# DLRM tower with a CIN stack on one core: six and four weight groups in odd tiles, all first-layer groups split, first-layer schedule moved

## What is computed

```python
def _cin_layer(X0, Xi, W, b):              # X0 [B,39,16], Xi [B,Fi,16], W [128, 39*Fi]
    Wr = W.reshape(H, F0_, Fi)
    return jnp.einsum('hjk,bjd,bkd->bhd', Wr, X0, Xi) + b[None, :, None]
X0 = e                                     # rows of 39 tables, gathered by ids
Xi = X0
for W, b in Ws:                            # three layers
    Xi = _cin_layer(X0, Xi, W, b)
    res.append(Xi.sum(axis=2))
z = jnp.concatenate(res, axis=1)           # [B, 384]
h = jnp.concatenate([z, dense_ctx], axis=1)
h = jnp.maximum(h @ W_top1 + b_top1, 0.0)
h = jnp.maximum(h @ W_top2 + b_top2, 0.0)
y = h @ W_top3
```

## Time and profile before

| | |
|---|---|
| Time, median of 3 runs | 663.59 us (663.03 to 664.0) |
| The profiled execution's own time | 664.12 us |
| Its span, first to last instruction | 662.2 us |
| Mean granted TensorE clock | 0.995 |
| TensorE busy | 648.3 us |
| VectorE busy | 558.7 us |
| GpSimd busy | 467.0 us |
| ScalarE busy | 441.9 us |

### The profile page before, as it was taken

How to read it: one execution, slowest core, us unless ns; L and a number is a source line. 1 busy time by engine, 2 the same in 40 slices (tenths; PEclk the granted TensorE clock), 3 DMA queues, 4 the chain that set the end, 5 groups by cost and what they waited for, 6 DMA issues and landing times.

```text
span 662.2 us, 11304 instructions
## 1 busy us (share of the span) xinstructions
PE 648.3 (98%) x3070; PEld 517.9 (78%) x3070; DVE 558.7 (84%) x1558; ACT 441.9 (67%) x1449; POOL 467.0 (71%) x376
## 2 busy tenths in 40 slices
PE   7898999999999999999999999999999999999998
PEld 6786678777788777777778877877778877777877
DVE  4669999999985799999995699999998489999980
ACT  3555678677763777777773577868675477777761
POOL 6888788888873688888875468787886377444540
PEclk9799999999999999999999999999999999999999
DMA  6023564040403004031221301313040300400000
GB/s 212 18 50 100 137 231 129 20 121 8 127 10 116 17 7 126 8 101 37 78 59 35 99 6 32 106 23 115 18 121 8 113 18 8 125 3 6 1 1 1
DMA packets 38356, 42.25 MB, mean 64 GB/s; under 512 B 17823, under 2 KB 22548, under 8 KB 38165
## 3 DMA queue, kind: packets, MB, share of 16 engines
q1 hardware_dynamic: 32661, 40.23, 20.0%
q0 software_dynamic: 5632, 1.31, 2.2%
HBM read 8.84 MB, written 0.00 MB: 13 GB/s over the span
## 4 chain that ended last, share of the span: by engine, by line
PE 94%; DVE 2%; DMA 2%; ACT 1%; issue 1%; POOL 1%; SPq 0%; POOLq 0%; DVEq 0%
PE p_u L820 22%; PE p_u L822 22%; PE p_u L821 22%; PE p_x L795 6%; PE p_tower L843 5%; PE p_g L834 5%; PE p_x L790 2%; PE p_x L789 2%; PE p_x L792 2%; DMA g_all<-w_in 1%; DVE z L611 1%; PE p_tower L870 1%; PE p_x L760 1%; PE p_x L772 1%; PE p_g L748 0%
## 5 line engine op out<-in xcount | busy, mean ns | idle before, releaser
L461 ACT ACTIVATE prod<-p_u,x0t 128x128 f32<-128x128 f32 x1024 | 290.4, 375 | 104.1 <-PE p_u L822 104.0
L652 DVE SCALAR_TENSOR_TENSOR parts<-p_u,x0t,parts 128x128 f32<-128x128 f32 x1024 | 283.9, 342 | 42.2 <-PE p_u L822 42.0
L820 PE MATMUL p_u<-w1h,x1h 128*128 128x512 f32 (+1 forms) x640 | 288.4, 451 | 0.8 <-ACT x1h L442 0.8
L822 PE MATMUL p_u<-w1h,x1l 128*128 128x512 f32 (+1 forms) x640 | 250.4, 391 | 0.0
L821 PE MATMUL p_u<-w1l,x1h 128*128 128x512 f32 (+1 forms) x640 | 250.1, 391 | 0.0
L339 POOL DMA_INDIRECT emb<-table_in,idx_all x176 | 205.6, 1168 | 49.8 <-issue 47.7
L358 POOL TENSOR_TENSOR parts<-parts,prod 128x512 f32<-128x512 f32 x128 | 176.9, 1382 | 53.3 <-ACT prod L461 39.9
L820 PEld LDWEIGHTS p_u<-w1h,x1h 128*128 128x128 f32 x640 | 120.9, 189 | 37.9 <-issue 8.2
L821 PEld LDWEIGHTS p_u<-w1l,x1h 128*128 128x128 f32 x640 | 121.5, 190 | 35.6 <-issue 10.8
L822 PEld LDWEIGHTS p_u<-w1h,x1l 128*128 128x128 f32 x640 | 120.7, 189 | 26.1
L353 POOL TENSOR_TENSOR parts<-prod 128x512 f32<-128x512 f32 x64 | 83.4, 1302 | 73.1 <-ACT prod L461 72.4
(11 more groups left out here) (87 smaller groups left out, 383.0 us busy)
## 6 DMA issues: line engine op xcount, KB each, us to landing
fac_b<-xx SPq DMA_DIRECT2D x90, 234.0 KB
fac_a<-xx SPq DMA_DIRECT2D x45, 78.0 KB
emb<-table_in,idx_all POOLq DMA_INDIRECT x176, 3.7
g_all<-w_in SPq DMA_DIRECT2D x3, 832.0 KB, 6.3
w<-w_in SPq DMA_DIRECT2D x1, 2496.0 KB, 9.2
xx<-xx SPq DMA_DIRECT2D x30, 78.0 KB
fac_b<-xx SPq DMA_DIRECT2D x15, 156.0 KB
bd<-x0t SPq DMA_DIRECT2D x120, 10.0 KB
```

The costliest lines, as they stand in the source:

```text
L461: last = nc.scalar.activation(dst[:, i * H:(i + 1) * H], u[:, i * H:(i + 1) * H], ACT.Copy, scale=x0t[:, par, t, j:j + 1])
L652: nc.vector.scalar_tensor_tensor(out=chain[i][:, p], in0=u[:, i * H:(i + 1) * H], scalar=x0t[:, par, t, j:j + 1], in1=add, op0=ALU.mult, o ...
L820: nc.tensor.matmul(u, xh, wh, start=True, stop=False)
L822: nc.tensor.matmul(u, xl, wh, start=False, stop=True).then_inc(u_full, 1)
```

## The change

It makes three moves.

- **Odd tiles are wide.** In odd tiles from T = 5 to T = 61 (29 tiles) ScalarE scales six quads (0, 2, 4, 5, 7, 9) and VectorE four (1, 3, 6, 8). `prod` gets a fifth buffer for them, GpSimd adds four times instead of three, and all counters become sums over tiles (`A_DONE`, `V_DONE`, `SUMS_DONE`).
- **All seven groups are split**, so groups 1, 3 and 5 too are handled in halves from macro 2 on.
- **The slots of the first layer move**: products to 0, 4, 8, ... 24, high halves 4 slots behind, low halves 6, adds 10 (10, 14, ... 34). The last add stays in slot 34.

```diff
-S_PAIR = [1 + 9 * k // 2 for k in range(GROUPS)]
-S_HIGH = [s + 1 for s in S_PAIR]
-S_LOW = [s + 3 for s in S_PAIR]
-S_ADD = [s + 6 for s in S_PAIR]
-SPLIT = (0, 2, 4, 6)
+S_PAIR = [4 * k for k in range(GROUPS)]
+S_HIGH = [s + 4 for s in S_PAIR]
+S_LOW = [s + 6 for s in S_PAIR]
+S_ADD = [s + 10 for s in S_PAIR]
+SPLIT = tuple(range(GROUPS))
...
-CHAIN_TILE = 20
-A_TILE = 5
-SUM_TILE = 3
+WIDE = [T % 2 == 1 and TILES < T < TILES_BLOCK * BLOCKS - 1 for T in range(TILES_BLOCK * BLOCKS)]
+A_QUADS = [(0, 2, 4, 5, 7, 9) if wide else (0, 2, 4, 6, 8) for wide in WIDE]
+V_QUADS = [(1, 3, 6, 8) if wide else (1, 3, 5, 7, 9) for wide in WIDE]
+A_DONE = [sum(map(len, A_QUADS[:T])) for T in range(len(WIDE) + 1)]
+V_DONE = [4 * sum(map(len, V_QUADS[:T])) for T in range(len(WIDE) + 1)]
+SUMS = [len(A_QUADS[T]) - 2 for T in range(len(WIDE))]
+SUMS_DONE = [sum(SUMS[:T]) for T in range(len(WIDE) + 1)]
+PRODS = [4, 5]
...
-        prod = sb("prod", [128, 2, 4, 4 * H])
+        prod = sb("prod", [128, sum(PRODS), 4 * H])
...
-                    pool.wait_ge(a_scaled, A_TILE * T + 3)
+                    pool.wait_ge(a_scaled, A_DONE[T] + 3)
...
-                    for i in (2, 3):
-                        pool.wait_ge(a_scaled, A_TILE * T + 2 + i)
-                        pool.wait_ge(summed, SUM_TILE * T + i - 1)
+                    for i in range(2, SUMS[T] + 1):
+                        pool.wait_ge(a_scaled, A_DONE[T] + 2 + i)
+                        pool.wait_ge(summed, SUMS_DONE[T] + i - 1)
...
-                        if q % 2 == 0:
+                        if q in A_QUADS[T]:
                             scale_quad(T, tt, q)
...
-                dve.wait_ge(chained, CHAIN_TILE * (T + 1))
-                dve.wait_ge(summed, SUM_TILE * (T + 1))
+                dve.wait_ge(chained, V_DONE[T + 1])
+                dve.wait_ge(summed, SUMS_DONE[T + 1])
...
-                        if q % 2 == 1:
+                        if q in V_QUADS[T]:
                             chain_quad(T, tt, q)
...
-                if q0 % 2 == 0:
-                    pe.wait_ge(a_scaled, A_TILE * T0 + q0 // 2 + 1)
+                if q0 in A_QUADS[T0]:
+                    pe.wait_ge(a_scaled, A_DONE[T0] + A_QUADS[T0].index(q0) + 1)
                 else:
-                    pe.wait_ge(chained, CHAIN_TILE * T0 + 4 * (q0 // 2 + 1))
+                    pe.wait_ge(chained, V_DONE[T0] + 4 * (V_QUADS[T0].index(q0) + 1))
```

More of the change, by code:

```diff
@@ L343, in pairs @@
             def pairs(p, i):
-                return prod[:, p, i, :].rearrange("p (a i h) -> p a i h", a=2, i=2)
+                return prod[:, p * PRODS[0] + i, :].rearrange("p (a i h) -> p a i h", a=2, i=2)
             def body(n, has_prev, has_next):
@@ L412, in evac_x0t @@
                     act.wait_ge(f_bd_in, 16 * TILE_B)
-                need(act, chained, CHAIN_TILE * TILES * (M - 1))
-                need(act, a_scaled, A_TILE * TILES * (M - 1))
+                need(act, chained, V_DONE[TILES * (M - 1)])
+                need(act, a_scaled, A_DONE[TILES * (M - 1)])
                 need(act, bd_in[par], 16 * TILE_B * pair)
@@ L453, in scale_quad @@
                 if q == 0:
-                    need(act, chained, CHAIN_TILE * (T - 2) + 4)
+                    if T > 1:
+                        act.wait_ge(chained, V_DONE[T - 2] + 4)
                     dst = start[:, p].rearrange("p a h -> p (a h)")
                 else:
-                    need(act, summed, SUM_TILE * (T - 2) + 3)
-                    dst = prod[:, p, q // 2 - 1, :]
+                    if T > 1:
+                        act.wait_ge(summed, SUMS_DONE[T - 1])
+                    dst = prod[:, p * PRODS[0] + A_QUADS[T].index(q) - 1, :]
                 u = p_u[(QUADS * tt + q) % RING]
@@ L639, in chain_quad @@
                 p, par, t = tt % 2, (tt // TILES) % 2, tt % TILES
-                k = q // 2
+                k = V_QUADS[T].index(q)
                 dve.wait_ge(u_full, QUADS * T + q + 1)
                 if k == 0:
-                    dve.wait_ge(a_scaled, A_TILE * T + 1)
+                    dve.wait_ge(a_scaled, A_DONE[T] + 1)
                     need(dve, x2_made, T - 1)
@@ L650, in chain_quad @@
                         add = chain[i][:, p]
-                        dve.wait_ge(chained, CHAIN_TILE * T + 4 * (k - 1) + i + 1)
+                        dve.wait_ge(chained, V_DONE[T] + 4 * (k - 1) + i + 1)
                     nc.vector.scalar_tensor_tensor(
```

## The result

The changed kernel takes **687.34 us** (686.79 to 687.91, 4 runs) against 663.8 (663.03 to 666.49, 4 runs): the ratio is 1.0348, with a 95% interval of 1.0319 to 1.0377. It is slower, as forecast, but by 23.5 us and not by 9: the time lies outside the range. The profiled execution took 686.79 us, 22.7 more than that of before; its span, 685.1 us, is 22.9 longer.

The account below looks back on a forecast made before the run. TensorE paces the kernel, with VectorE and GpSimd within 2 us. Profiled 664.1 - 6.3 (splitting) + 15.4 (VectorE stalling TensorE in 11 steady macros) = 673.2, so 672.7 us measured; range 658.5 to 684.

Parts of the forecast that it names:

- Splitting saves 0.15 us a group: TensorE, groups 1, 3 and 5 in 14 macros: 0.70 instead of 0.85 us each, 6.3 us saved if TensorE paces.
- VectorE's work of 32.8 us: VectorE, a macro after the change: 32.8 us of work for 34.8 us, about 1 us left for everything else.
- Products and low halves exclude GpSimd's sums: VectorE's products and low halves and GpSimd's sums cannot run together; a hit waits 0.47 us on average.
- The size of the collisions: VectorE waiting for GpSimd's sums, per macro: 0.7 us with the luck of before, 3.8 at random; 2.4 taken.
- Less the 1.0 of margin, a stall of 1.4 us: 2.4 us of collisions less 1.0 of VectorE's margin: 1.4 us per steady macro, 11 macros, +15.4 us.
- In the three tower macros VectorE has 15 us to spare, and the saving stands: Macros 4, 8 and 12: no stall counted, the splitting saving kept, tower macros 0.4 us shorter.
- Whatever delays VectorE in the first third lands on TensorE: Low half 1, ahead of group 1's third matmul: margin 0, so delays reach TensorE in full; later, anything over 1.0 us.
- GpSimd's fourth sum costs nothing beyond collisions: GpSimd, odd tiles: demand 37.2 us per macro, but the lag is stored and tower macros clear it; no cost beyond collisions.
- the copies cost nothing: SyncE's fac_b copies: needed one to four slots earlier, but issued some 3 us ahead of the next macro; no cost.
- Rival 3: GpSimd becomes the bound, folds wait for sums: 667.4 us, or 679.4 with no store; chance 0.20.
- ScalarE costs nothing: ScalarE: two quads and three high halves more per macro, 26.6 to about 30 of 35 us, hidden by its waits.
- Rival 1: TensorE keeps pacing, collisions 0.7 us with some 0.2 per macro reaching TensorE: 659.5 us, 657.3 with none; chance 0.25.

Follow-up runs that it names:

- e3: The kernel after with GpSimd's sums adding only 4 of every 128 columns (output not the reference's): 656.65 us, against 663.71 for the kernel before on that chip.
- e14: The kernel after with GpSimd's sums replaced by MEMSETs that write and read nothing (sums left out): 662.2 us, steady macros 34.7 us.
- e2: The kernel after without wide tiles (all groups split, new slots, three sums in every tile): 690.32 us.
- e12: The kernel after (wide odd tiles, all groups split) with the old slots: 705.55 us.
- e5: The kernel after with VectorE's z1 sum moved from slot 1 to slot 31: steady macros of 36.0, 36.2 and 37.6 us.
- e6: The kernel after with the z1 sum in slot 31, adds one slot later and the fold in slot 8 instead of 7: 704.66 us.
- e13: The kernel after with a tile's gathers issued ahead of its sums instead of behind: 694.06 us on another chip; macros 5 to 7 take 35.2, 37.0, 37.1 us.
- e8: The kernel before with one more group split, group 3: 672.8 against 673.26 us, ratio 0.9991 (0.9958 to 1.0024).
- e10: The kernel before with groups 3 and 5 split too, old slots, no wide tiles: 678.69 us, ratio 1.0084 (1.0047 to 1.0121).
- e11: The kernel before with all seven groups split, old slots, no wide tiles: 688.93 us.
- e1: The kernel after with the old split and old slots, so only the wide odd tiles are left of the change: 677.24 us.

## Why the prediction was wrong in size

- **TensorE paces before, with two engines close behind: right.** Splitting saves 0.15 us a group: right; e3 shows 0.5 us a macro, where 0.45 was forecast.
- **VectorE's work of 32.8 us: right** (32.7 to 32.9 in every variant with the same quads and low halves).
- **Products and low halves exclude GpSimd's sums: right**, shown by e3 and e14.
- **The size of the collisions: wrong.** "I take 2.4" was a choice between a lucky 0.7 and a random 3.8 us per macro. The 11 steady macros show 3.2 on average (1.8 to 4.5). That this is near the random end is chance: it is not made of 8 hits of 0.47 us but of 3 to 5 of 0.65 on average (0.25 to 1.8), because a product recorded just ahead of a sum can lose too, and then waits for all of it. The same count for e2 and e12 would give 3.1 and 3.5, and they show 1.9 and 2.0.
- **"Less the 1.0 of margin, a stall of 1.4 us": wrong in size.** e3's macros against after's give 2.05 us on average, 22.5 us in eleven macros instead of 15.4 (1.4 of them are the late copy of macro 2). The margin was about right (VectorE's idle time falls from 2.0 to 0.8 us on average, so 1.2 us is absorbed). 7.1 us of the miss.
- **"In the three tower macros VectorE has 15 us to spare, and the saving stands": wrong, and against the prediction's own finding.** The tower's matmuls run in slots 15 to 35; the stall stands at slots 6 to 14, where a tower macro is like any other. Macro 4 loses 0.23 us at slot 6, 0.69 at 12 and 1.75 at 14. The three together last 155.9 us and in e3 148.8: 2.4 us each. Another 7.1 us of the miss. The steps add up: the forecast was 9.1 us, the two misses are 7.1 each, macro 0 is 1.5, and the saving that e3 shows against before, 5.7 us in the steady macros and 2.5 in the towers, is 1.9 us more than the 6.3 forecast; that gives the 22.9 us of the spans.
- **"Whatever delays VectorE in the first third lands on TensorE": right in place**, all stalls stand at slots 6 to 14; but as a cause it misled. e5 and e6 show that in macros such as 6 and 7 it is VectorE's whole macro that is full. There the place only says where the debt is collected.
- **GpSimd's fourth sum costs nothing beyond collisions, and the copies cost nothing: right but for macro 2.** Folds wait for sums nowhere in after, and e13 moves macros by 1.1 to 1.3 us either way at the same work. Rival 3 is out. But the fourth sum puts the gathers later, and in macro 2 a product waits 2.4 us for the copy that follows them; the prediction took its "some 3 us ahead" from macro 5, while the first copy of `fac_b` in macro 1 is issued only 2.0 us ahead of the next macro before, and 0.6 us behind its start after. That GpSimd is nearly full is true all the same: its waits for data, 1.8 us in macro 6 before, are 0 to 0.6 us in the steady macros from 2 to 11.
- **ScalarE costs nothing: right for the change as made**, and only thanks to its new slots, which e12 shows. The forecast had not asked what the old slots would have done.
- **Rival 1** would have needed stalls under 0.55 us. The luck of before did not return: its products were held noticeably once a macro, in macros 5 to 7, those of after three to five times.
- Macro 0's 1.5 us go with the clock, as far as the two traces show, and are no part of any step.

## What to carry to other kernels

When two engines exclude each other, the sum to compare with the bound is work plus collisions, and the collisions of a tuned kernel are a property of its phases. Here they stayed low (0.4 to 0.9 us in macro 6) while slots and sums stayed as they were, even with one to three low halves more (e8, e10, e11), and rose with the new slots (e2, 1.9) and with the wide tiles (e1, 1.8). Do not carry the low number over to a change that moves either; a count for random starts gives only its order of size. If a queue is full over a whole stage, more slack at the place where the stall shows does not help; look for what fills the queue. And before a saving is counted in a stage that has spare time, check in which slots the spare time lies.

## What the hardware showed beyond that

**Who comes first is not settled by the recorded start.** The product at 312.56 is recorded 0.15 us ahead of the sum at 312.71 and waited for all of it; that at 321.65 by 0.13 us. In the kernel before one with a lead of 0.48 us did so (GpSimd's two rows, then VectorE's):

```profile
66.89 1.00 POOL L339 DMA_INDIRECT emb<-table_in,idx_all  x1 [0.30 <-issue]
67.92 1.29 POOL L353 TENSOR_TENSOR parts<-prod 128x512 f32<-128x512 f32 x1
...
67.44 2.32 DVE L611 TENSOR_TENSOR z<-fac_b,fac_a 78x512 f32<-78x512 f32 x1
```

What these have in common is a gather that still runs when VectorE's instruction starts, with the sum 0.02 to 0.03 us behind the gather. Twelve traces have sums of all 512 columns. In them a product, low half or x1l is recorded 0.01 to 0.61 us ahead of a sum 620 times. With a gather running at its start (leads of 0.03 to 0.59 us) it waited for the whole sum 62 of 63 times. With the gather over before it starts (0.01 to 0.56) it never did, 117 of 117, and behind another sum neither, 440 of 440. Why a running gather decides it stays open. The Trainium skill (the same page and section) has it that issue order, not op shape, decides who blocks. By the profile's starts that does not hold while a gather runs.

**Gathers are held up as well.** In macro 7 of after, a gather of GpSimd takes 1.00 us where VectorE is at its quads, and 1.25 where a low half ran with it:

```profile
319.20 1.25 POOL L346 DMA_INDIRECT emb<-table_in,idx_all  x1 [0.18 <-issue]
320.75 1.00 POOL L346 DMA_INDIRECT emb<-table_in,idx_all  x1 [0.30 <-issue]
```
